# A two-layer recurrent block: the AV product of layer 0 turned round, the queries divided before the scores, prefix states from one PSUM bank, and the expert weight put on the input of each expert

## The reference, cut to what matters

```
Q, K = relu(rope(x@wq)), relu(rope(x@wk)); V = x@wv     # 16 heads of 8
numerator   = Q . cumsum(K (x) V)     # over the positions of a batch
denominator = Q . cumsum(K)
s = (numerator / (denominator + 1e-6)) @ wo

scores = softmax(x @ Wg.T); w = top 2 of 8, normalised   # cw[t, e]
h = silu(x @ W1[e].T) * (x @ W3[e].T)                    # 352 hidden per expert
g = sum over e of cw[t, e] * (h @ W2[e].T)
```

## Time and profile before

| | us |
|---|---|
| median of 3 executions | 1771.62 |
| lowest, highest | 1755.31, 1772.21 |
| the profiled execution | 1760.05 |
| its span, first to last instruction | 1758.2 |
| prologue, to the first copy of `xn0T` | 106.2 |
| first pass with units | 112.6 |
| the six full passes, each | 132.5, 133.1, 136.9, 133.6, 139.4, 140.1 |
| last pass | 83.6 |
| second stage | 640 |

### The profile page before, as it was taken

One profiled execution on the slowest core, in us unless ns is written; L12 is line 12 of the kernel. 1 busy time (PEld: TensorE's weight loads), 2 busy tenths in 40 slices (PEclk: granted clock), 3 DMA queues, 4 the chain that ended last, 5 costly groups with the idle time before them and its releaser, 6 DMA issues. The chain is left out here.

```text
span 1758.2 us, 20407 instructions
## 1 busy us (share of the span) xinstructions
PE 1402.3 (80%) x6256; PEld 835.0 (47%) x6256; DVE 984.9 (56%) x2806; ACT 510.1 (29%) x938; POOL 554.0 (32%) x574
## 2 busy tenths in 40 slices
PE   3789979978979978979997998515997777777853
PEld 2444434434435434434443443203796666666753
DVE  2344575585675676576557567573007546855571
ACT  0021131131121131131131121114875654555530
POOL 0000016016016006106105204352016556566565
PEclk9998988898988898898898899757998889888985
DMA  8900021021021021021020020315864444444331
GB/s 275 355 19 1 0 78 42 0 78 42 1 75 46 1 72 39 9 72 39 9 66 33 15 66 29 121 39 179 277 214 125 138 123 127 136 131 131 122 90 42
DMA packets 123093, 152.11 MB, mean 87 GB/s; under 512 B 15262, under 2 KB 82270, under 8 KB 122231
## 3 DMA queue, kind: packets, MB, share of 16 engines
q1 hardware_dynamic: 106614, 117.39, 20.8%
q0 software_dynamic: 16384, 33.59, 6.6%
HBM read 73.33 MB, written 77.60 MB: 86 GB/s over the span
## 5 line engine op out<-in xcount | busy, mean ns | idle before, releaser
L1021 POOL DMA_INDIRECT y<-y_rows,idxy x256 | 267.8, 1046 | 280.2 <-DMA y_rows<-ys 132.1
L988 POOL DMA_INDIRECT rows<-xn,idx x256 | 255.1, 996 | 84.0 <-issue 82.5
L633 PE MATMUL U<-xn0T,wff 128*128 128x512 f32 x352 | 206.8, 672 | 53.2 <-DVE hs L1331 53.2
L859 ACT ACTIVATE hs<-GY 128x512 f32<-128x512 f32 x176 | 104.7, 595 | 482.1 <-PE GY L627 374.0
L646 PE MATMUL ACC<-hw,wff 128*128 128x512 f32 x352 | 209.7, 688 | 0.0
L627 PE MATMUL GY<-xn0T,wff 128*128 128x512 f32 x352 | 202.7, 660 | 6.6 <-DVE xn0T L1325 6.6
L962 POOL TENSOR_TENSOR rs<-rs,neg_half 128x4 f32<-128x4 f32 x16 | 16.4, 1024 | 588.9 <-DVE rs L1059 588.9
L1331 DVE TENSOR_TENSOR hs<-hs,U 128x512 f32<-128x512 f32 x176 | 120.6, 685 | 136.3 <-PE U L633 83.8
L1406 DVE SCALAR_TENSOR_TENSOR pos<-neg,pos 128x1024 f32<-128x1024 f32 x8 | 9.8, 1225 | 255.4 <-ACT neg L914 168.7
L554 PEld LDWEIGHTS V<-vaug,att 128*128 128x128 f32 x1024 | 148.8, 233 | 5.7 <-DVE att L1140 4.9
L1336 DVE TENSOR_TENSOR hw<-hs,B 128x512 f32<-128x512 f32 x176 | 121.0, 688 | 48.7 <-PE B L639 33.1
(11 more groups left out here) (260 smaller groups left out, 2158.5 us busy)
## 6 DMA issues: line engine op xcount, KB each, us to landing
xg<-rows SPq DMA_DIRECT2D x104, 256.0 KB
y_rows<-ys SPq DMA_DIRECT2D x104, 256.0 KB
rows<-zero SPq DMA_DIRECT2D x7, 2048.0 KB, 9.4
rows<-zero SPq DMA_DIRECT2D x1, 12288.0 KB, 53.6
wff<-in_wgz SPq DMA_DIRECT2D x2, 3840.0 KB, 38.6
wd<-in_wd SPq DMA_DIRECT2D x1, 5120.0 KB, 24.3
wff<-in_w SPq DMA_DIRECT2D x3, 1408.0 KB, 9.1
rows<-xn,idx POOLq DMA_INDIRECT x256
```

What stands on the lines that cost most here:

```text
L633: nc.tensor.matmul(U[:, :], w3_0[:, u * P:(u + 1) * P], xn0T[:], start=True, stop=True).then_inc(sem["up_ps"], 1)
L859: nc.scalar.activation(hs[:, u % 2, :], G[u % 2][:, :], ACT.Silu).then_inc(sem["silu_ready"], 1)
L988: pool.indirect_dma_start(rows, bass.IndirectOffsetOnAxis(ap=idx[:, t * 8 + k:t * 8 + k + 1], axis=0), xn1[:, t, :], None)\
L1021: pool.indirect_dma_start(y8[:, i % RG, k, :], None, y_d[0:groups * Q * P, :], bass.IndirectOffsetOnAxis(ap=idxy[:, b, t * 8 + k:t * 8 + k ...
```

## The change

Five things change in layer 0. **Units:** the product by `B` and the 22 broadcasts of L639 go. Once for each expert e, PE broadcasts its weights over 128 rows, and DVE makes `xw`, the input times that weight; the up product then takes `xw` as moving data. A unit that has two experts is cut into pieces of 32, 64 or 128 rows of output (`segments`), each with its expert's `xw`. These broadcasts and the up products share `U` and `B` as a ring of two banks: product k waits only until product k-2 has been read. **Division:** all four subtiles get q, k, v first, `s_cum` makes the running sum of k for all positions in `V`, and DVE divides q by q . cumsum(k) before anything is turned. **States:** `s_outer` makes the three prefix states in one bank from three products, and DVE masks them once. **AV:** v stands in `vpad` as weights of 32 columns, four heads to a column group with zeros around, and the scores move; the outputs of all subtiles are added in `V`, already turned. `s_o_norm`, `s_o_T` and `state` go. **ACT** makes `qm` (four copies with a scale) and `vpad` (four copies). The steps move with it: attention starts at step 30, its subtiles are 10 steps apart, and the token weights (`s_weights`) are cut in two. Small inputs change: `sel0` shrinks, `onesf` is new, the columns of wv and rows of wo are in another order.

```diff
+def segments(u):
+    made, p = [], 0
+    while p < P:
+        e = (u * P + p) // HID0
+        end = min(P, (e + 1) * HID0 - u * P)
+        n = next(n for n in (128, 64, 32) if p % n == 0 and p + n <= end)
+        made.append((p, p + n, e))
+        p += n
+    return made
+BROADCAST = {0: [1]}
+for e in range(2, E0):
+    BROADCAST.setdefault(first_unit(e) - 2, []).append(e)
...
+         23: ["place_a"], 25: ["place_b"], 28: ["place_c"], 29: ["scatter"], 38: ["kp"], 39: ["cum", "outer"], 40: ["den_a"],
+         41: ["states", "den_b"], 72: ["cw0_T", "cw0T_copy"], 82: ["oT_copy"], 84: ["wo"], 85: ["s0"]}
 for t in range(T):
-    for at, name in ((0, "qkv0"), (1, "rope"), (3, "qk_T"), (4, "qkT_copy"), (6, "scores_a"), (7, "mask_a"),
-                     (9, "scores_b"), (10, "mask_b"), (11, "av"), (12, "o_norm"), (14, "o_T"), (14, "oT_copy")):
-        STEPS.setdefault(31 + 13 * t + at, []).append((name, t))
+    for at, name in ((30 + 2 * t, "qkv0"), (31 + 2 * t, "rope"), (43 + 10 * t, "qk_T"), (44 + 10 * t, "qkT_copy"),
+                     (46 + 10 * t, "scores_a"), (47 + 10 * t, "mask_a"), (48 + 10 * t, "scores_b"), (49 + 10 * t, "mask_b"),
+                     (51 + 10 * t, "av"), (45 + 10 * t, "weights_a"), (50 + 10 * t, "weights_b")):
...
+            def s_cum(t):
+                pe.wait_ge(*seen.next("qk0_ready", T))
+                reuse("V")
+                nc.tensor.matmul(V[:, :], causal[:], qk[:, 1, :, :].rearrange("p t d -> p (t d)"), start=True, stop=False, skip_group_check=True)
+                nc.tensor.matmul(V[:, P:2 * P], onesf[:], qk[:, 1, 0, :], start=False, stop=False, skip_group_check=True)
+                pe.wait_ge(*seen.next("kp_ready"))
+                nc.tensor.matmul(V[:, 2 * P:4 * P], onesf[:], kp[:].rearrange("p t d -> p (t d)"), start=False, stop=True, skip_group_check=True)\
...
+            def s_outer(t):
+                qkv0_read()
+                for s in range(T - 1):
+                    n = T - 1 - s
+                    last = nc.tensor.matmul(X0[:, s * D:(T - 1) * D].rearrange("p (n d) -> p n d", d=D), qk[:, 1, s, :],
+                                            v0[:, s, :].unsqueeze(1).broadcast_to([P, n, D]), start=(s == 0), stop=(s == T - 2),
...
             def s_scores_a(t):
...
-                if t:
-                    pe.wait_ge(*seen.next("state_ready"))
-                    reuse("V")
-                    nc.tensor.matmul(V[:, 0:H * HA], qkT[:, 0:P], state[:], start=True, stop=False, skip_group_check=True)
+                nc.tensor.matmul(V[:, t * P:(t + 1) * P], states[:, t, :], qkT[:, 0:P], start=(t == 0), stop=False, skip_group_check=True)
...
             def s_av(t):
-                for h in range(H):
-                    last = nc.tensor.matmul(V[:, h * HA:(h + 1) * HA], att[:, h // 4, (h % 4) * P:(h % 4 + 1) * P], vaug[:, h, :],
-                                            start=(t == 0 and h == 0), stop=(h == H - 1), skip_group_check=True)
+                for g in range(4):
+                    for r in range(4):
+                        last = nc.tensor.matmul(V[32 * r:32 * r + 32, t * P:(t + 1) * P], vpad[:, g, r, :], att[:, g, r * P:(r + 1) * P],
+                                                start=False, stop=(g == 3), skip_group_check=True)
...
+                def taken(k):
+                    if item + k > 0:
+                        pe.wait_ge(sem["ring_read"], seen.value("ring_read", item + k))
...
-                        nc.tensor.matmul(U[:, :], w3_0[:, u * P:(u + 1) * P], xn0T[:], start=True, stop=True).then_inc(sem["up_ps"], 1)
+                        k = ITEM_UP[u]
+                        taken(max([k - 1] + [ITEM_CW[e] + 1 for _, _, e in segments(u)]))
+                        for p0, p1, e in segments(u):
+                            last = nc.tensor.matmul((U, B)[k % 2][p0:p1, :], w3_0[:, u * P + p0:u * P + p1], xw[:, e % 2, :], start=True, stop=True)
...
-                        nc.tensor.matmul(B[:, :], sel0[:, u * P:(u + 1) * P], cw0T[:], start=True, stop=True).then_inc(sem["b_ps"], 1)
+                        for e in BROADCAST.get(u, []):
+                            broadcast(e)
...
             def s_qkT_copy(t):
                 copy(qkT[:], X1[:, 0:2 * P], "qkT0_ps", "qkT0_ready")
+                for r in range(4):
+                    last = nc.scalar.activation(qm[:, r, :], X1[:, 0:P], ACT.Copy, scale=headm[:, r:r + 1])
+                last.then_inc(sem["qm_ready"], 1)
+                for g in range(4):
+                    last = nc.scalar.activation(vpad_v[:, g, :, g, :], v0[:, t, :].rearrange("p (r c m) -> p r c m", r=4, c=4)[:, :, g, :], ACT.Copy)
...
+            def s_den_a(t):
+                dve.wait_ge(*seen.next("cum_ps"))
+                nc.vector.tensor_tensor(attf[:, 0:T * D], qk[:, 0, :, :].rearrange("p t d -> p (t d)"), V[:, :], ALU.mult).then_inc(sem["cum_read"], 1)
+                dve.wait_ge(*seen.next("cum_read"))
+                link(nc.vector.tensor_reduce(dn[:], attf[:, 0:T * D].rearrange("p (c m) -> p c m", m=HD), AX.X, ALU.add))
...
+                def scaled(e):
+                    dve.wait_ge(*seen.next("ring_ps"))
+                    nc.vector.tensor_tensor(xw[:, e % 2, :], xn0T[:], (U, B)[ITEM_CW[e] % 2][:, :], ALU.mult).then_inc(sem["ring_read"], 1)
...
-                        nc.vector.tensor_tensor(hw[:, u % RH, :], hs[:, u % 2, :], B[:, :], ALU.mult).then_inc(sem["hw_ready"], 1)
+                        for e in BROADCAST.get(u, []):
+                            scaled(e)
```

More of the change, by code:

```diff
@@ L106, in loop_end, with first_unit @@
         self.reg = None
+def first_unit(e):
+    return e * HID0 // P
+def segments(u):
[10 more added lines that the diff above has]
+    BROADCAST.setdefault(first_unit(e) - 2, []).append(e)
+ITEM_UP, ITEM_CW = {}, {0: 0}
+for u in range(U0):
+    ITEM_UP[u] = len(ITEM_UP) + len(ITEM_CW)
+    for e in BROADCAST.get(u, []):
+        ITEM_CW[e] = len(ITEM_UP) + len(ITEM_CW)
 STEPS = {0: ["res_silu"], 1: ["res_gate"], 3: ["res_T"], 4: ["res_add"], 6: ["res_norm"], 9: ["xn1_T", "res_r1"],
@@ new lines, in s_qkv0, with qkv0_read @@
+                if t >= 2:
+                    qkv0_read()
+                nc.tensor.matmul(ps[bank][:, 0:3 * D], xn0Tn[:, t * P:(t + 1) * P], wqkv0[:], start=True, stop=True)\
+                    .then_inc(sem["qkv0_ps"], 1)
+                seen.readers[bank] = []
+            def qkv0_read():
+                pe.wait_ge(*seen.next("rope_ready"))
+                pe.wait_ge(*seen.next("v0_ready"))
+            def s_cum(t):
[5 more added lines that the diff above has]
+                nc.tensor.matmul(V[:, 2 * P:4 * P], onesf[:], kp[:].rearrange("p t d -> p (t d)"), start=False, stop=True, skip_group_check=True)\
+                    .then_inc(sem["cum_ps"], 1)
+                seen.readers["V"] = ["cum_read"]
@@ L620, in f0, with broadcast @@
                     pe.wait_ge(*seen.next("rot_ready"))
+                item = seen.count["ring_read"]
+                def taken(k):
+                    if item + k > 0:
+                        pe.wait_ge(sem["ring_read"], seen.value("ring_read", item + k))
+                def broadcast(e):
+                    k = ITEM_CW[e]
+                    taken(k - 1)
+                    nc.tensor.matmul((U, B)[k % 2][:, :], sel0[:, e * P:(e + 1) * P], cw0T[:], start=True, stop=True).then_inc(sem["ring_ps"], 1)
                 for s in range(4 * (U0 + LAG)):
                     u, part = divmod(s, 4)
+                    if units and s == 0:
+                        broadcast(0)
                     if units and u < U0 and part == 0:
@@ L644, in f0 @@
                             reuse("ACC")
-                        pe.wait_ge(*seen.next("hw_ready"))
-                        nc.tensor.matmul(ACC[:, :], w2_0[:, v, :], hw[:, v % RH, :], start=(v == 0), stop=(v == U0 - 1))\
+                        taken(ITEM_UP[v] + 1)
+                        nc.tensor.matmul(ACC[:, :], w2_0[:, v, :], hs[:, v % RH, :], start=(v == 0), stop=(v == U0 - 1))\
                             .then_inc(sem["acc_done" if v == U0 - 1 else "down_done"], 1)
@@ L649, in f0 @@
                 if units:
+                    seen.next("ring_read", ITEMS)
                     seen.readers["ACC"] = ["gT0_ready"]
@@ L856, in f0 @@
                         act.wait_ge(*seen.next("g_ps"))
-                        if u >= 2:
-                            act.wait_ge(*seen.next("hw_ready"))
-                        nc.scalar.activation(hs[:, u % 2, :], G[u % 2][:, :], ACT.Silu).then_inc(sem["silu_ready"], 1)
+                        if u >= RH:
+                            act.wait_ge(*seen.next("down_done"))
+                        nc.scalar.activation(hs[:, u % RH, :], G[u % 2][:, :], ACT.Silu).then_inc(sem["silu_ready"], 1)
                     others(STEPS, s, want)
                 if units:
-                    seen.next("hw_ready", 2)
+                    seen.next("down_done", RH - 1)
```

(21 more changed lines are left out.)

155 lines of the change are left out of this document (78 added, 77 removed), and 1 row of the table STEPS.

## The result

| | before, us | changed, us |
|---|---|---|
| median of 4 executions each | 1771.91 | 1607.4 |
| lowest, highest | 1755.31, 1775.85 | 1602.66, 1617.64 |
| the profiled execution, its span | 1760.05, 1758.2 | 1617.64, 1615.5 |
| prologue and first pass with units | 218.8 | 183.2 |
| six full passes, mean | 135.9 | 117.6 |

In the spans: -35.6 in prologue and first pass (forecast -28), -110.1 in the full passes (-104), -2.8 in the last (-4), +5.8 in the second stage (0). That sum is -142.7 against a forecast of -136.

What follows compares the result with a forecast made beforehand. PE was taken to bound the first stage. Six full passes at -17.4 (-104), first pass -12, last -4 and prologue -16 sum to -136: 1624 against 1760.05, with the median put at 1628 us, range 1585 to 1700.

Steps and rivals of the forecast that it cites:

- Bound: First stage: PE sets the time, busy 118 to 122 of 133 to 137 us in full passes, DVE 86.
- the products that are gone: Full pass: three outer products, three of the state's part and four transposes go, -2.7 us.
- Broadcasts, -7.8: Units of a full pass: 22 expert-weight broadcasts become 8, -2.8 us in units 0 to 7, -5.0 in 8 to 21.
- Cut up products, +3.4: Up products of two-expert units: +3.4 us a full pass, equal widths sharing time, a 64 ahead of two 32; ends +0.8, +6.7.
- AV, -8.1: Attention's AV products in a full pass: 14.5 us falls to 6.4, at 1.4 plus 0.2 for changes each; ends -9, +0.7.
- The third rival: AV and cut pieces: column groups take turns and the clock stays low, 1795 us, slower; chance 0.06.
- New products, +3.8: Full pass: sums of k 1.5 us, three outer products 1.3, four products with `states` at 0.25 each.
- The clock, -10: Full pass: of 33 us at 1.2 GHz, 10 stay after the DVE wait, 23 go with AV; ends -12, 0.
- New waits, +4: Full pass: PE waits for the division chain 2 us, ACT's copies before silu, and `xw` 0.5; ends 0, +10.
- The place wait stays: Full pass: PE's 6.73 us wait for DVE remains, as ring product 7 still needs DVE's read of 6.
- The other passes: Outside the six full passes: first pass with units -12 us, last pass -4, prologue -16.
- The clock doesn't come back: Full passes: the new AV leaves the clock low, so a pass gains only 7.4 us, 1690 in total; chance 0.15.

Runs made afterwards that it cites:

- E9: The changed kernel unaltered, run again on another chip beside two variants, against the kernel before: 1545.84 us, ratio 0.882.
- E4: The changed kernel with units of three pieces cut into four pieces of 32 rows: 1599.67 us, ratio 0.909 to the kernel before.
- E2: The kernel before with the new units but the old attention: 1707.85 us, ratio 0.969 to the kernel before.
- E3: The changed kernel with AV's two loops exchanged, four products in a row writing one column group: 1642.2 us, ratio 0.930 to the kernel before.
- E7: The changed kernel with expert 3's broadcast moved from unit 6 to unit 5: 1548.46 us, ratio 0.883 to the kernel before.
- E6: The changed kernel with AV's products in two steps and a unit's product between: 1546.91 us, ratio 0.883 to the kernel before.
- E1: The changed kernel with the new attention but the old units, a broadcast for each unit: 1635.29 us, ratio 0.927 to the kernel before.

## Why the prediction was right, and where it was not

The forecast's total came out, 1607 for 1628, and its steps on PE's work did too. But the trace that it was set against contains a delay that it didn't know of, and where that delay is absent the kernel takes 1546 us, below the range. That the total came out is in part luck, as three sums for a mean full pass show. Each is PE's work at full clock, half of the time at 1.2 GHz, and PE's idle time:

| | work | half of low | idle | pass, us |
|---|---|---|---|---|
| kernel before | 103.8 | 16.8 | 15.4 | 135.9 |
| forecast | 92.4 | 6.8 | 19.4 | 118.5 |
| changed, first trace | 93.8 | 9.7 | 14.1 | 117.6 |
| changed, E9 | 93.5 | 3.4 | 9.0 | 105.9 |

The late signal put in some 11 us a pass, about as much as the forecast had set aside for waits and low clock that the change itself doesn't have. Point by point, for a full pass:

- **Bound.** PE before and after. Taking half of each low stretch off its busy time, PE's work is 120.6 - 33.6 / 2 = 103.8 us before and 103.4 - 19.3 / 2 = 93.8 after (means of the six), so -10; the forecast of its terms, without clock and waits, was -11.4. The terms as measured below, with the broadcasts and the products that are gone as forecast, come to -11.5; the 1.5 between isn't traced.
- **Broadcasts, -7.8.** A unit's products now start 0.86 apart each and the broadcast's slot is gone, as counted. The part under DVE, in units 0 to 7, isn't measured by itself.
- **Cut up products, +3.4.** Right, with the guess on widths: (1.99 - 0.86) x 3 + 0.15 = 3.5, and 0.1 to 0.2 more in the product ahead of each cut unit, so about 4. The starts at 246.91 to 248.37 show the guess at work, the 64 ahead of the two 32, and E4 shows what it costs.
- **AV, -8.1.** Mis-sized: 1.4 us was taken, 0.81 measured, 1.01 to the next product. From 3.51 before (404.32 to 407.83) that is -2.5 four times, -10.0, or -9.6 with the 0.1 that the product ahead loses. The forecast took the earlier trace rows as 0.073 us a pass, from eight passes with their run-in; their single starts lie in pairs, 0.109 us apart. So a pass in one column group comes every 0.109 us, with 64 columns of weights there and 32 here, and two or four groups do it side by side: eight rounds, 0.9 us. The third rival was right that such a pass costs 0.1 us, and wrong that groups take turns. The Trainium skill, TensorE: Matmul & The Clock Gate, LDWEIGHTS, gives a load of 32 columns an estimated 27 ns, and 0.81 / 31 is 26 ns a pass; but the rounds show no load every 27 ns, so the trace doesn't bear this out as the cause. The Trainium skill, TensorEngine Tiling (Array Packing), Key Properties, says that a change of tiling mode drains the engine; the trace has about 0.1 us for it on either side of AV, 0.95 for the product ahead (243.89 to 244.84) instead of 0.86, and as much behind the last round, together the forecast's own 0.2.
- **New products, +3.8.** 2.94 us for sums and outer products (2.8 counted), 0.42 for each product with `states` (0.25 counted): +4.6.
- **The clock, -10.** The forecast let 10 us at 1.2 GHz stay behind the place wait and 23 go with the old AV. That holds: 6.8 us stay there, in both traces of the change, and the idle-free stretches of the old attention are gone. What the forecast didn't know are the 12.5 us a pass more in the first trace, of which all but two short stretches of 3.4 us (behind waits of 0.6 and 1.0 us) follow the late signal's waits, and which E9 doesn't have. Not all of the 23 was AV's either: 15.4 was, by the count under E2. What in the old AV lowers the clock stays open; E3 excludes only a length of 2.2 us.
- **New waits, +4.** This step failed. None of those named shows in E9: in its six full passes PE waits at the place steps, for the norm (L509 and L522) and for the new batch at the head of a pass, and for nothing else. The first trace adds one wait of 2.4 to 5.5 us a pass, for `qm`, that comes from the late signal, and 4.2 us in all six passes for masks and `kp`. Waits of the kernel before (up to 2.6 us, two or three a pass, around each subtile's products) are gone as well: PE is idle 9.0 us a pass where it was 15.4 before and the forecast kept 19.4. That is 10.4 of the 12.6 us between 118.5 forecast and 105.9 in E9. Some of the kernel before's waits stand behind its own late signals, and no trace of it without them exists, so how many the change itself removes isn't shown.
- **The place wait stays.** Right, 5.7 to 6.2 for 6.73, and E7 shows that the ring is not its only cause.
- **The other passes.** Prologue: transposes at 42.67 (43), periods of 10.8, 11.2 and 11.6 (11.7), first work of the units at 90.1 (92). The forecast's own terms for a period, 20 - 4.1 - 4.3 - 0.6 + 0.3, add up to 11.3 and not to 11.7, which is most of the 2 us. By the copies, which bound the passes in the table, the prologue is 20.7 us shorter, 4.7 more than forecast. The first pass is 3 us shorter than forecast, for AV and waits again. **The second stage** was put at 0 and is 5.8 us longer in the first trace, 9.8 in E9. Its time at 1.2 GHz went from 231 to 233 and 251 us. Half of the 20 more would be E9's difference, but E6 has the same 251 us in a stage of 646; nothing here shows the cause.

Of the rivals, turns of the column groups didn't happen, but E3 shows part of them to be real, and how near they were: an exchange of two loops. "The clock doesn't come back" was half true in the first trace, by another cause, and not in E9. What stays open is the late signal: it is there in the traces of two comparisons, the first and E1 to E4, in the kernel before and all variants, always beside the scatter, and in none of the traces of three later ones, on two other chips than that of E1 to E4. Whether the chip, the moment or something else decides isn't shown. No trace of the kernel before exists for those later ones. Between its two traces the changed kernel loses 11.7 us a pass (5.2 of waiting, and half of 12.5 us at the lower clock), 70 in all. The kernel before went from 1772 to 1749 only, so the ratio moves from 0.910 to 0.882.

## What to carry to other kernels

A small product, one with few columns of weights or few moving, cost 0.11 us a pass here whichever of the two was few. What made it cheap was to have four of them side by side: write neighbours in order to different column groups, count rounds and not products, and cut pieces to one width. When a wait names an engine whose own rows say that it was done long ago, compare the consumer's start with the producer's in another trace of the same kernel before a cause is looked for in the order. And run the unaltered kernel in each comparison: here four edits seemed to cure what was absent anyway.

## What the runs showed of the hardware that was not expected

- 32 passes of 128 columns with 32 columns of weights in four column groups take 0.81 us from first to last start when neighbours differ in group, in rounds of four that are 0.109 us apart; 2.19 us when four products in a row share one (E3).
- A pass of 9 moving columns on 128 columns of weights comes every 0.112 us, one of 128 on 64 (two groups) or on 32 (four groups) every 0.109 in its group.
- Stretches at 1.2 GHz that begin with PE busy all the time stand in or right behind the old AV, 17 in the kernel before and 16 in E2, and in no kernel with the new one.
- A piece of 64 columns of weights and two of 32, each with 512 moving columns, take 1.99 us; four of 32 take 1.00, two of 64 1.01.
- On some executions PE's results after a burst of AV products reach ACT and DVE 1 to 9 us late (8.84 in E1) while GpSimd writes rows by index, with PE's own rows unchanged to 0.02 us; on others never.
